# Delta-rule attention in one core: the order of VectorE's work in a slot, and who gates the output row

## The chip, the cores and the metric

The kernel runs on one core of a Trainium2 chip. The metric is the device time of one execution in microseconds. Every duration below comes from one profiled execution of the kernel before.

## The reference

Six residual layers act on x of shape (2, 2048, 256): a gated feed-forward, the delta-rule attention, the feed-forward again, a binary-weight layer, a state-space layer, and the binary layer again. The change is in the attention. For each head (16 heads of size 16) and each chunk of 64 tokens:

```python
q = l2norm(x @ Wq) / sqrt(K); k = l2norm(x @ Wk); v = x @ Wv; gate = x @ Wg
P = where(strict, (k_beta @ k.T) * L, 0)          # L: decays exp(g_i - g_j)
Ainv = I + P + P@P ... ; v = Ainv @ v; k_cumdecay = Ainv @ (k_beta * exp(g))
# scan over the chunks, with state S
attn = where(tril, (q @ k.T) * L, 0)
v_new = v - k_cumdecay @ S
o = (q * exp(g)) @ S + attn @ v_new
S = S * exp(g_last) + (k * exp(g_last - g)).T @ v_new
# afterwards
o = o * rsqrt(mean(o*o) + 1e-5) * norm_w;  o = o * silu(gate);  out = o @ Wo
```

The kernel works in chunks of 32 rows instead of 64, which is the same mathematics.

## The kernel before

The program is a row of phases: first feed-forward, gates, delta (the attention), feed-forward, binary, space, binary. Only `delta_sync`, `delta_vector` and `delta_gpsimd` are touched.

The 4096 rows are 32 tiles of 128 rows (64 from each sequence; four sub-chunks of 32 rows, two steps of the scan in time). The delta phase runs 40 slots, n = 0 to 39. It is a software pipeline written out by hand: in slot n the projections and normalised keys of tile n are made, the decays and the masked products of tile n-1 (`LAG_FORM`), the inverse is applied for tile n-6, the scan runs for tile Z = n-7 (`LAG_SCAN`), and the output projection runs for tile O = n-8 (`LAG_OUT`). `at(stage, t)` calls a stage if tile t exists. Each engine has its own loop over n, so the order of the calls in it is the order of its queue; engines meet only through semaphores.

**VectorE** (`delta_vector`, L1818 to L1845) has two kinds of work. The first is the triangular solve (`solve`, L1741): for each pair of tiles 58 steps, 29 (`HALF_SOLVE`) per slot, each of which waits for the step before it through `S.i_step`. Even slots do the first half, in which the operations grow from 30 columns to 240; odd slots the second, in which they shrink again. The second kind is the stages, put between the steps:

- `sum_qk` (L1695), sum of the squares of q and k; `scale_qk` (L1709), normalises q and k out of PSUM bank 4 into `QK`;
- `faded_q` (L1717), from PSUM bank 1; it waits for `f_kt`, which ScalarE's `keep_kq` (L1585, L1586) raises;
- `keep_gate` (L1701); `keep_within` and `keep_attn` (L1726, two operations each);
- the scan: `own_heads` (L1784) twice per slot, waiting for `s_b` from TensorE's `to_state` (L1474), and `new_state` (L1792, L1797) twice;
- the output: `sum_o` (L1803), `scale_o` (L1808), `add_o` (L1812), and for the first 12 tiles `new_stats` (L312, L313).

**GpSimd** (`delta_gpsimd`, L1900 to L1909): `fade_first` (L1882), `middle_state` (L1889), `fade_second` (L1894), `gate_o` (L1898), `decayed_k` (L1865), `kept_k` (L1875, two operations). All of them read SBUF. The last two wait for `scale_qk` through `p_kn`.

**TensorE** (`delta_tensor`, L1515 to L1531) is not touched. Its order in slot n is: `from_values`, `from_state` (L1442, L1461) for Z half 0, `project_qk(n)` (L1371), `to_state` (L1474) half 0, `turn_kq(n-1)` (L1401), `decays` (L1389, L1392), `from_values` and `from_state` half 1, `project_vg` (L1381), `to_state` half 1, `turn_o` (L1506), `apply` (L1427), `outputs` (L1492, L1497), `within` (L1411), `project_o` (L1512). The waits that matter:

```python
def project_qk(t):
    pe.wait_ge(S.p_in[t % 2], 16 * (t // 2 + 1))
    if t > 0:
        pe.wait_ge(S.p_kn, t)          # scale_qk(t - 1) has read bank 4
```

`turn_kq(t)` waits for `scale_qk(t)` too, and `outputs` for `keep_gate` and both halves of the state.

**ScalarE**, in slot n: `keep_y` (L1626) and `widen` (L1642) half 0, `squares(n)` (L1541), `keep_kq(n-1)`, DMA issues, `keep_y` half 1, `root_qk` (L1553, L1554), `widen` half 1, `keep_v`, `sigmoid_g`, `exp_decays`, `keep_ot`, `keep_wt`, `keep_ut`, `keep_o`, `spread_vk`, `root_o`.

**SyncE** sends and fetches the scratch tensors: `keys_out` writes the scaled keys of a tile and `keys_in` brings them back in another layout, seven tiles deep.

Of the kernel before, what the change touches and what calls it, by code (L numbers as in the profile page):

```python
# [8 lines left out]
ALU = mybir.AluOpType  # L9
# [10 lines left out]
BLK = 4  # L20
NT = 32
# [28 lines left out]
def bcast_last(ap, n):  # L50
    return ap.unsqueeze(2).to_broadcast([ap.shape[0], ap.shape[1], n])
# [6 lines left out]
def heads(ap):  # L58
    return ap.rearrange("p (h d) -> p h d", d=HD)
# [223 lines left out]
AHEAD = 3  # L283
# [902 lines left out]
LAG_FORM, LAG_PAD, LAG_APPLY, LAG_SCAN, LAG_OUT = 1, 5, 6, 7, 8  # L1186
# [67 lines left out]
def solve_count(m, k):  # L1254

    return m * (2 * HALF_SOLVE + 1) + 1 + k
# [7 lines left out]
def at(stage, t, *more):  # L1264

    if 0 <= t < NT:
        stage(t, *more)


def turned_in(e, B, xT, S, t):  # L1270

    b = t // BLK
    e.wait_ge(S.xt_out[b % 2], 32 * (b // 2 + 1))
    src = bass.AP(tensor=B.xT_dram, offset=t * P, ap=[[NT * P, P], [P * NT * P, KD], [1, P]])
    e.dma_start(xT[t % 2].rearrange("p (k n) -> p k n", k=KD), src).then_inc(S.p_in[t % 2], 16)
# [14 lines left out]
def delta_sync(e, B, M, S, run):  # L1290
    Pd, Td = B.P_dram, B.T_dram

    def rows_in(t):
        if t >= 2:
            e.wait_ge(S.p_vg, t - 1)
            turned_in(e, B, M.xT, S, t)

    def decays_in(t):
        if t >= 2:
            e.wait_ge(S.f_d, t - 1)  # L1300
            e.wait_ge(S.f_qgt, t - 1)
        e.wait_ge(S.g_out, 48)
        for part in range(2):
            rows = bass.AP(tensor=B.g_dram, offset=part * NT * NH * P + t * NH * P, ap=[[512, 4], [1, 512]])
            e.dma_start(M.G[t % 2][4 * part:4 * part + 4, :], rows).then_inc(S.f_in[t % 2], 16)
        for g in range(G2):
            src = bass.AP(tensor=B.eg_dram, offset=(t * NH + 8 * g) * P, ap=[[P, 8], [0, HD], [1, P]])
            e.dma_start(M.egT[t % 2][:, g * P:(g + 1) * P], src).then_inc(S.f_in[t % 2], 16)

    def keys_out(t):  # L1310
        e.wait_ge(S.p_kd, t + 1)
        dst = bass.AP(tensor=B.Kd_dram, offset=t * P * DM, ap=[[SUB, P], [SUB * P, 8], [1, SUB]])
        e.dma_start(dst, M.Kd_tok[t % 2].rearrange("p (n c) -> p n c", n=8)).then_inc(S.k_out[t % 2], 16)

    def keys_in(t):

        e.wait_ge(S.k_out[t % 2], 16 * (t // 2 + 1))
        if t >= 2:
            e.wait_ge(S.k_in[t % 2], 64 * (t // 2))
        if t >= 7:  # L1320
            e.wait_ge(S.s_b, 2 * (t - 6))
        for r in range(4):
            src = bass.AP(tensor=B.Kd_dram, offset=t * P * DM + 8192 * r, ap=[[SUB, SUB], [1024, 8], [1, SUB]])
            dst = M.Kd[t % 7][SUB * r:SUB * r + SUB, :].rearrange("p (n c) -> p n c", n=8)
            e.dma_start(dst, src).then_inc(S.k_in[t % 2], 16)

    def pair_in(m):
        e.wait_ge(S.i_out[0], 64 * (m + 1))
        e.wait_ge(S.i_out[1], 64 * (m + 1))
        if m >= 2:  # L1330
            e.wait_ge(S.i_back[m % 2], 16 * (m // 2))
        whole = bass.AP(tensor=Pd, offset=m * 131072, ap=[[1024, P], [1, 1024]])
        e.dma_start(M.PR[m % 2], whole).then_inc(S.i_in[m % 2], 16)

    def pair_back(m):
        back = bass.AP(tensor=Td, offset=m * 131072, ap=[[1024, P], [1, 1024]])
        e.wait_ge(S.i_step, solve_count(m, 2 * HALF_SOLVE))
        e.dma_start(back, M.PR[m % 2]).then_inc(S.i_back[m % 2], 16)

    def within_out(t):  # L1340
        e.wait_ge(S.f_pt, t + 1)
        for r in range(4):
            dst = bass.AP(tensor=Pd, offset=t * 65536 + r * 16384, ap=[[SUB, SUB], [1024, NH], [1, SUB]])
            e.dma_start(dst, M.PT[SUB * r:SUB * r + SUB, :].rearrange("p (n i) -> p n i", n=NH)).then_inc(S.i_out[t % 2], 16)

    for n in range(SLOTS):
        at(rows_in, n + 1)
        at(decays_in, n)
        at(keys_out, n - 1)
        at(keys_in, n - 2)  # L1350
        at(within_out, n - LAG_FORM)
        if n % 2 == 0:
            if 0 <= (n - 2) // 2 < NT // 2:
                pair_in((n - 2) // 2)
            if 0 <= n - 5 < NT:
                inverse_in(e, B, M, S, n - 5, (0, 1), S.i_diag)
        elif 0 <= (n - 5) // 2 < NT // 2:
            pair_back((n - 5) // 2)
            inverse_in(e, B, M, S, n - 5, (0, 1), S.i_diag)
# [327 lines left out]
def delta_vector(v, own, B, M, S, run):  # L1687
# [117 lines left out]
    def scale_o(t):  # L1805
        v.wait_ge(S.o_rs, t + 1)
        v.wait_ge(S.o_sb, t + 1)
        v.tensor_tensor(heads(M.o_sb), heads(M.o_sb), bcast_last(M.o_rs, HD), ALU.mult).then_inc(S.o_mul, 1)  # L1808

    def add_o(t):  # L1810
        v.wait_ge(S.o_w, t + 1)
        v.tensor_tensor(B.X[:, t, :], bank[7][:, DM:], B.X[:, t, :], ALU.add).then_inc(S.o_x, 1)  # L1812
# [5 lines left out]
    for n in range(SLOTS):  # L1818
        Z, O = n - LAG_SCAN, n - LAG_OUT
        at(own_heads, Z, 0)  # L1820
        solve(n, 0, 1)
        at(new_state, Z, 0)
        solve(n, 1, 3)
        at(sum_qk, n)
        solve(n, 3, 6)
        at(faded_q, n - LAG_FORM)
        solve(n, 6, 10)
        at(scale_qk, n)
        solve(n, 10, 11)
        at(own_heads, Z, 1)  # L1830
        solve(n, 11, 12)
        at(new_state, Z, 1)
        solve(n, 12, 15)
        at(keep_gate, n)
        solve(n, 15, 21)
        at(sum_o, Z)
        solve(n, 21, 24)
        at(keep_within, n - LAG_FORM)
        solve(n, 24, 25)
        at(keep_attn, n - LAG_FORM)  # L1840
        solve(n, 25, 29)
        at(scale_o, Z)
        at(add_o, O)
        if O < AHEAD * BLK:
            at(new_stats, O)  # L1845


def delta_gpsimd(g, own, B, M, S, run):
# [34 lines left out]

    def middle_state(t):
        g.wait_ge(S.s_e, 2 * t + 1)
        g.wait_ge(S.s_bm, 2 * t + 1)
        if t > 0:
            g.wait_ge(S.s_wide, 2 * t)
        g.tensor_tensor(M.S1, M.E0, M.Bm, ALU.add).then_inc(S.s_1, 1)  # L1889
# [3 lines left out]
        g.wait_ge(S.s_1, t + 1)  # L1893
        g.tensor_tensor(states(M.E1), states(M.S1), bcast_last(end[:, 4:8], SUB), ALU.mult).then_inc(S.s_e, 1)  # L1894

    def gate_o(t):
        g.wait_ge(S.o_mul, t + 1)
        g.tensor_tensor(M.o_sb, M.o_sb, M.gate[t % 9], ALU.mult).then_inc(S.o_gate, 1)  # L1898

    for n in range(SLOTS):  # L1900
        Z = n - LAG_SCAN
        at(fade_first, Z)
        at(middle_state, Z)
        at(fade_second, Z)
        at(gate_o, n - LAG_OUT)
        at(decayed_k, n)
        at(kept_k, n)
        if n in (SLOTS - 4, SLOTS - 3):
            first_factors(g, own, B, S, 1, n - (SLOTS - 4))  # L1909

# [273 lines left out]
```

## Time and profile before

| | us |
|---|---|
| profiled execution, device time | 1235.57 |
| its span on the core | 1233.8 |
| the three timed runs | 4384.79, 3293.92, 1240.54 |
| their median | 3293.92 |
| delta phase, about | 222 to 825 of the span |

The span is what the profile shows, from the first to the last instruction. Over the whole span TensorE is busy 84%, VectorE 75%, ScalarE 49%, GpSimd 33%; these are averages over phases with different limits, and the delta phase, half of the span, has to be read by itself.

### The profile page before, as it was taken

The numbers are of one execution on the slowest core, as the hardware profiler recorded it, in microseconds if no ns is written. First come the engines' busy times: TensorE is split into PE (matmuls) and PEld (weight loads), VectorE is DVE, ScalarE is ACT, GpSimd is POOL, SyncE is SP. The second block draws the span as 40 slices with busy tenths as digits, with TensorE's granted clock in tenths as the row PEclk, the third lists the DMA queues.
The fourth block names the chain that finished last, engine by engine and source line by source line (L and its number), as shares of the span: only waits on it lengthen the run. The fifth ranks groups of instructions, "written<-read, shape, count | busy, mean of one in ns | idle before, by whom it ended". The sixth has DMA issues, their size and how long they took to land. (4 is left out here: it accounts for less than half of the span.)

```text
span 1233.8 us, 38552 instructions
## 1 busy us (share of the span) xinstructions
PE 1038.0 (84%) x15542; PEld 739.6 (60%) x15542; DVE 925.7 (75%) x2403; ACT 599.7 (49%) x1614; POOL 405.8 (33%) x580
## 2 busy tenths in 40 slices
PE   2999977778888888788898886679999798799878
PEld 2888853445555565555565565458888574355455
DVE  3777736358999999999988988528776345899853
ACT  2433336434767676777766765554332452101052
POOL 2666630311222121222121211216665257400055
PEclk9999988886999999999989987779999798899979
DMA  9000013244444444444434443100000034954013
GB/s 251 20 2 1 1 27 141 69 87 98 104 101 103 94 97 86 102 106 104 100 78 99 102 94 71 42 2 1 1 1 1 18 74 104 232 160 115 1 35 103
DMA packets 282625, 93.31 MB, mean 76 GB/s; under 512 B 208976, under 2 KB 275408, under 8 KB 282448
## 3 DMA queue, kind: packets, MB, share of 16 engines
q1 hardware_dynamic: 247056, 84.03, 28.3%
q10 hardware_dynamic: 35392, 6.82, 2.9%
q8 instruction: 123, 2.02, 0.7%
q14 instruction: 54, 0.44, 0.1%
HBM read 56.20 MB, written 30.41 MB: 70 GB/s over the span
## 5 line engine op out<-in xcount | busy, mean ns | idle before, releaser
L1777 DVE TENSOR_TENSOR delta_tmp<-delta_PR 128x130 f32<-128x130 f32 (+12 forms) x416 | 152.9, 368 | 9.4
L1774 DVE TENSOR_TENSOR delta_PR<-delta_PR,delta_tmp 128x130 f32<-128x130 f32 (+12 forms) x416 | 152.1, 366 | 9.3
L1889 POOL TENSOR_TENSOR delta_S<-delta_E,delta_Bm 128x128 f32<-128x128 f32 x32 | 15.3, 477 | 282.2 <-issue 273.3
L1427 PE MATMUL psum<-delta_T,delta_pad 128*32 128x128 f32 x2048 | 81.2, 325 | 31.9 <-DMA delta_T<-inverse_scratch 31.4
L1626 ACT ACTIVATE delta_y<-psum 32x128 f32<-32x128 f32 x256 | 68.7, 268 | 80.1 <-PE psum L1461 58.2
L1427 PEld LDWEIGHTS psum<-delta_T,delta_pad 128*32 128x32 f32 x2048 | 69.6, 131 | 41.7 <-DMA delta_T<-inverse_scratch 38.2
L507 POOL TENSOR_TENSOR ffn_H<-ffn_hid,ffn_H 128x512 fp32r<-128x512 f32 x48 | 61.8, 1292 | 57.5 <-DVE ffn_H L473 57.5
L1642 ACT ACTIVATE delta_wide<-delta_S 32x128 f32<-32x128 f32 x256 | 78.2, 306 | 3.2
L507 POOL TENSOR_TENSOR first_H<-first_hid,first_H 128x512 fp32r<-128x512 f32 x48 | 61.7, 1292 | 53.9 <-DVE first_H L473 53.9
L1411 PE MATMUL psum<-delta_MV,delta_KT 32*32 32x128 f32 x2048 | 68.9, 287 | 10.6 <-ACT delta_E L1576 10.6
L1865 POOL TENSOR_TENSOR delta_VK<-delta_QK,both_eg 128x256 f32<-128x256 f32 x32 | 20.8, 650 | 156.6 <-DVE delta_QK L1709 156.5
L1411 PEld LDWEIGHTS psum<-delta_MV,delta_KT 32*32 32x32 f32 x2048 | 58.9, 112 | 22.2 <-ACT delta_E L1576 15.5
L1371 PE MATMUL psum<-both_w_in,delta_xT 128*128 128x512 f32 x128 | 67.0, 648 | 3.3 <-DVEq L172 2.1
L439 ACT ACTIVATE first_silu<-psum 128x512 f32<-128x512 f32 x48 | 28.7, 599 | 84.2 <-PE psum L392 84.2
L439 ACT ACTIVATE ffn_silu<-psum 128x512 f32<-128x512 f32 x48 | 28.8, 599 | 81.3 <-PE psum L392 81.3
L641 PE MATMUL psum<-w_bin,binary_XT 128*128 128x256 f32 x256 | 67.4, 408 | 0.0
L312 DVE BATCH_NORM_STATS2 ln_stats<-X 128x6 f32<-128x256 f32 x128 | 54.1, 423 | 17.0 <-DMA X<-in_x 14.4
L1474 PEld LDWEIGHTS psum<-delta_y,delta_Kd 32*32 32x32 f32 x2048 | 22.9, 110 | 71.0 <-ACT delta_y L1626 71.0
L1381 PE MATMUL psum<-both_w_in,delta_xT 128*128 128x512 f32 x128 | 64.4, 627 | 0.0
L710 DVE TENSOR_SCALAR binary_Y<-psum 128x512 f32<-128x512 f32 x32 | 22.1, 692 | 54.5 <-PE psum L641 54.5
L392 PE MATMUL psum<-first_XT,w_gate 128*128 128x512 f32 x192 | 54.6, 407 | 3.7 <-DVE first_XT L461 3.7
L641 PEld LDWEIGHTS psum<-w_bin,binary_XT 128*128 128x128 f32 x256 | 48.4, 199 | 14.2 <-issue 8.4
(282 smaller groups left out, 2594.8 us busy)
## 6 DMA issues: line engine op xcount, KB each, us to landing
within_scratch<-delta_PT SPq DMA_DIRECT2D x128, 64.0 KB, 1.9
delta_PR<-within_scratch SPq DMA_DIRECT2D x16, 512.0 KB, 4.3
inverse_scratch<-delta_PR SPq DMA_DIRECT2D x16, 512.0 KB, 3.0
space_T<-taps_scratch SPq DMA_DIRECT2D x8, 1024.0 KB, 5.9
X<-taps_scratch SPq DMA_DIRECT2D x8, 1024.0 KB, 8.9
X<-in_x SPq DMA_DIRECT2D x32, 128.0 KB, 10.2
turned_scratch<-gates_XT SPq DMA_DIRECT2D x16, 256.0 KB, 2.3
delta_xT<-turned_scratch SPq DMA_DIRECT2D x32, 128.0 KB, 3.8
```

Source lines behind the costliest of these rows:

```text
L392: i = pe.matmul(bank[:], w[:, k * HID + m * P:k * HID + (m + 1) * P].bitcast(F32R), M.XT[b % 2][hl][k].bitcast(F32R), start=(k == 0 and hl ...
L439: a.activation(M.silu[n % 3], B.bank[n % 2][:], ACT.Silu, scale=1.0 / 127.0).then_inc(S.silu, 1)
L507: g.tensor_tensor(lo.bitcast(F32R), M.hid[n % 3], hi, ALU.subtract).then_inc(S.hid_lo, 1)
L641: i = pe.matmul(o[:, j * DM:(j + 1) * DM], M.XT[b % 3][k][:, (2 * h + j) * P:(2 * h + j + 1) * P], B.w_bin[:, k * DM:(k + 1) * DM], start= ...
L1371: i = pe.matmul(bank[4][:], M.xT[t % 2][:, k * P:(k + 1) * P], M.w_in[:, k, 0:512], start=(k == 0), stop=(k == 1))
L1381: i = pe.matmul(bank[5][:], M.xT[t % 2][:, k * P:(k + 1) * P], M.w_in[:, k, 512:1024], start=(k == 0), stop=(k == 1))
L1411: mm = pe.matmul(kk[g][rows, q * P:(q + 1) * P], M.KT[rows, g * P + SUB * q:g * P + SUB * q + SUB], M.MV[rows, (4 * g + q) * P:(4 * g + q ...
L1427: i = pe.matmul(bank[3][SUB * c:SUB * c + SUB, (2 * w + g) * P:(2 * w + g + 1) * P], M.pad[:, from_c:from_c + SUB], M.T[t % 2][:, h * P:(h ...
L1626: i = a.activation(dst, heads(bank[6][rows, half * P:(half + 1) * P]), ACT.Copy)
L1642: i = a.activation(states(M.wide[half])[rows, :, SUB * c:SUB * c + SUB], states(X)[rows, :, :], ACT.Copy)
L1774: i = v.tensor_tensor(after, after, t3, ALU.add)
L1777: i = v.tensor_tensor(t3, column.to_broadcast([P, j, n_after]), row.to_broadcast([P, j, n_after]), ALU.mult)
```

## The change

In the slot loop of `delta_vector`, `scale_qk` goes from a third of the way through the solve to behind it, and `keep_within` and `keep_attn` go behind it too. `faded_q`, `sum_qk` and `add_o` (now of tile O-1, a slot later) go ahead of the solve, directly behind the first half of the state update. Ten places inside the solve where a stage stood become four. `gate_o` moves from GpSimd to VectorE, at the slot's end. GpSimd's `fade_first` for the next tile goes to the end of its slot, and its `middle_state` waits for the second operation of VectorE's state update (`s_x`) rather than the first (`s_bm`). SyncE's `keys_out` and `keys_in` come one slot later.

```diff
--- before.py
+++ after.py
@@ delta_sync
-        at(keys_out, n - 1)
-        at(keys_in, n - 2)
+        at(keys_out, n - 2)
+        at(keys_in, n - 3)
@@ delta_vector
+    def gate_o(t):
+        v.wait_ge(S.o_mul, t + 1)
+        v.tensor_tensor(M.o_sb, M.o_sb, M.gate[t % 9], ALU.mult).then_inc(S.o_gate, 1)
+
     for n in range(SLOTS):
         Z, O = n - LAG_SCAN, n - LAG_OUT
         at(own_heads, Z, 0)
-        solve(n, 0, 1)
         at(new_state, Z, 0)
-        solve(n, 1, 3)
+        at(add_o, O - 1)
+        at(faded_q, n - LAG_FORM)
         at(sum_qk, n)
-        solve(n, 3, 6)
-        at(faded_q, n - LAG_FORM)
-        solve(n, 6, 10)
+        if O - 1 < AHEAD * BLK:
+            at(new_stats, O - 1)
+        solve(n, 0, 9)
+        at(own_heads, Z, 1)
+        solve(n, 9, 10)
+        at(new_state, Z, 1)
+        solve(n, 10, 15)
+        at(keep_gate, n)
+        solve(n, 15, 25)
+        at(sum_o, Z)
+        solve(n, 25, 29)
         at(scale_qk, n)
-        solve(n, 10, 11)
-        at(own_heads, Z, 1)
-        solve(n, 11, 12)
-        at(new_state, Z, 1)
-        solve(n, 12, 15)
-        at(keep_gate, n)
-        solve(n, 15, 21)
-        at(sum_o, Z)
-        solve(n, 21, 24)
         at(keep_within, n - LAG_FORM)
-        solve(n, 24, 25)
         at(keep_attn, n - LAG_FORM)
-        solve(n, 25, 29)
         at(scale_o, Z)
-        at(add_o, O)
-        if O < AHEAD * BLK:
-            at(new_stats, O)
+        at(gate_o, Z)
+    add_o(NT - 1)
@@ delta_gpsimd
     def middle_state(t):
         g.wait_ge(S.s_e, 2 * t + 1)
-        g.wait_ge(S.s_bm, 2 * t + 1)
+        g.wait_ge(S.s_x, 2 * t + 1)
@@
-    def gate_o(t):
-        g.wait_ge(S.o_mul, t + 1)
-        g.tensor_tensor(M.o_sb, M.o_sb, M.gate[t % 9], ALU.mult).then_inc(S.o_gate, 1)
-
     for n in range(SLOTS):
         Z = n - LAG_SCAN
-        at(fade_first, Z)
         at(middle_state, Z)
         at(fade_second, Z)
-        at(gate_o, n - LAG_OUT)
         at(decayed_k, n)
         at(kept_k, n)
+        at(fade_first, Z + 1)
```

## Rows read from the trace of the kernel before

**Rows 1.** Windows of the delta phase: us, each engine's busy us, PEclk, DMA.

```profile
263.00:307.00 44.00, 33.12 (x401) 20.18 (x399) 39.27 (x114) 17.80 (x51) 5.17 (x10) 0.77 0.41 89
...
323.00:729.00 406.00, 345.51 (x9334) 232.57 (x9333) 375.48 (x1093) 286.44 (x911) 90.76 (x168) 0.97 0.46 97
```

**Rows 2.** VectorE's waits from 323 to 729: total us, times, longest.

```profile
DVE delta_Bm L1784 <- PE psum L1474: 5.6, 12, 0.9
```

**Rows 3.** Timeline: the solve's first steps without and with GpSimd beside them.

```profile
263.65 0.69 DVE L1763 SCALAR_TENSOR_TENSOR delta_PR<-delta_PR 128x30 f32<-128x30 f32 x3
...
595.28 1.07 DVE L1763 SCALAR_TENSOR_TENSOR delta_PR<-delta_PR 128x29 f32<-128x29 f32 x2
...
595.58 0.73 POOL L1898 TENSOR_TENSOR delta_o_sb<-delta_o_sb,delta_gate 128x256 f32<-128x256 f32 x1
```

**Rows 4.** Timeline of VectorE: two chained steps, then a stage between two steps.

```profile
604.64 0.39 DVE L1777 TENSOR_TENSOR delta_tmp<-delta_PR 128x220 f32<-128x220 f32 x1
...
605.07 0.39 DVE L1774 TENSOR_TENSOR delta_PR<-delta_PR,delta_tmp 128x220 f32<-128x220 f32 x1
605.37 0.41 DVE L1803 TENSOR_REDUCE delta_o_ss<-delta_o_sq 128x16 f32<-128x256 f32 x1
605.70 0.38 DVE L1777 TENSOR_TENSOR delta_tmp<-delta_PR 128x228 f32<-128x228 f32 x1
```

**Rows 5.** Groups of VectorE, 222 to 830: count | busy us, mean ns | idle before.

```profile
L1777 DVE TENSOR_TENSOR delta_tmp<-delta_PR 128x130 f32<-128x130 f32 (+12 forms) x416 | 152.9, 368 | 9.4
L1774 DVE TENSOR_TENSOR delta_PR<-delta_PR,delta_tmp 128x130 f32<-128x130 f32 (+12 forms) x416 | 152.1, 366 | 9.3
...
L1763 DVE SCALAR_TENSOR_TENSOR delta_PR<-delta_PR 128x29 f32<-128x29 f32 (+1 forms) x48 | 23.8, 521 | 0.6
L1709 DVE TENSOR_TENSOR delta_QK<-psum,delta_rs 128x512 f32<-128x512 f32 x32 | 22.0, 687 | 8.1 <-ACT delta_rs L1554 7.8 <-issue 0.2
L1695 DVE TENSOR_REDUCE delta_ssq<-delta_sq 128x32 f32<-128x512 f32 x32 | 21.6, 676 | 9.4 <-ACT delta_sq L1541 9.4
L1784 DVE TENSOR_TENSOR delta_Bm<-psum,consts 128x128 f32<-128x128 f32 x64 | 18.1, 283 | 18.1 <-PE psum L1474 18.1
...
L1808 DVE TENSOR_TENSOR delta_o_sb<-delta_o_sb,delta_o_rs 128x256 f32<-128x256 f32 x32 | 13.4, 419 | 2.5 <-ACT delta_o_rs L1561 2.5
...
L1768 DVE SCALAR_TENSOR_TENSOR delta_PR<-delta_PR 128x29 f32<-128x29 f32 (+1 forms) x48 | 11.7, 273 | 1.1
L312 DVE BATCH_NORM_STATS2 ln_stats<-X 128x6 f32<-128x256 f32 x12 | 5.1, 427 | 0.4
```

**Rows 6.** Timeline of early slots: scaled keys to projection, turned keys to faded_q.

```profile
230.45 0.69 DVE L1709 TENSOR_TENSOR delta_QK<-psum,delta_rs 128x512 f32<-128x512 f32 x1 [0.65 <-ACT delta_rs L1554]
...
231.29 1.95 PE L1371 MATMUL psum<-both_w_in,delta_xT 128*128 128x512 f32 x4 [1.19 <-DVE delta_QK L1709]
...
242.28 0.60 PE L1401 MATMUL psum<-consts,delta_QK 128*128 128x128 f32 x4
...
244.54 0.42 DVE L1717 TENSOR_TENSOR delta_QgT<-psum,delta_egT 128x256 f32<-128x256 f32 x1 [0.74 <-ACT delta_KT L1586]
```

**Rows 7.** Timeline of a full slot's start: TensorE from the outputs on, VectorE's wait.

```profile
689.08 0.65 PE L1492 MATMUL psum<-delta_y,delta_AT 128*32 128x64 f32 x32 [1.01 <-DVE delta_gate L1701]
...
693.72 1.98 PE L1371 MATMUL psum<-both_w_in,delta_xT 128*128 128x512 f32 x4
...
695.64 0.45 PE L1474 MATMUL psum<-delta_y,delta_Kd 32*32 32x32 f32 x32
...
696.02 0.66 PE L1401 MATMUL psum<-consts,delta_QK 128*128 128x128 f32 x4
...
696.17 0.29 DVE L1784 TENSOR_TENSOR delta_Bm<-psum,consts 128x128 f32<-128x128 f32 x1 [0.85 <-PE psum L1474]
```

**Rows 8.** Window (columns as in rows 1) and timeline of a stretch at granted clock 0.50.

```profile
285.00:289.00 4.00, 4.00 (x50) 2.65 (x43) 3.69 (x12) 0.00 (x0) 0.22 (x1) 0.50 0.03 4
...
287.38 3.06 PE L1371 MATMUL psum<-both_w_in,delta_xT 128*128 128x512 f32 x4
```

## Prediction

> **What bounds the kernel now.** I read the windows by phase first. In the part of the delta phase where every stage runs, 323 to 729, 24 slots take 406.0 us, 16.92 each; VectorE is busy 375.5 of them (92%) and TensorE 345.5 (85%) [rows 1]. So VectorE's queue sets the slot, with TensorE close behind. Then the waits: what VectorE loses to others in that stretch is small, 12 waits of at most 0.9 us for `to_state` among them [rows 2]. Last, the timeline, for what is inside the 92%: the solve's first operations are stretched when GpSimd reads SBUF beside them. Three of them take 0.69 us together in slot 4, where GpSimd is quiet, and in slot 24, with `gate_o` of 0.73 us beside them, two take 1.07 [rows 3].
>
> **The change part by part.** I give costs per slot; there are 24 full slots, n = 8 to 31.
>
> *Contention, removed.* The four solve lines are busy 152.9 + 152.1 + 23.8 + 11.7 = 340.5 us [rows 5], 10.64 per slot. The 48 operations of L1763 have the size of those of L1768 (273 ns), yet average 521 [rows 5]; without a neighbour three take 0.69 us, 0.23 to 0.25 each [rows 3]. That excess is 48 x 0.27 = 13 us, 0.4 per slot. The wider steps beside `decayed_k` and `kept_k`, and `new_state`, I put at as much again (the other SBUF-to-SBUF steps of the same half slots), so 0.9 per slot from the solve and 0.3 from `new_state`: 1.2 removed. Bounds: 0.4, L1763 alone, and 2.0. Behind the change GpSimd's operations lie beside PSUM-reading stages, which show no stretch (`scale_qk` 687 ns, `own_heads` 283 [rows 5]), except for `scale_o` and `gate_o`; I leave 0.3 for those two.
>
> *Interleaving, lost.* A chained step starts 0.43 us after a step of 0.39: its duration and 0.04. With `sum_o` (0.41) between them the two steps are 0.63 apart, so the stage costs 0.20 [rows 4]: an operation that waits for nothing starts about 0.08 before the end of the one ahead of it, and hides the 0.03 to 0.04 of the next wait. Each place where a stage breaks the chain is worth 0.11. Ten places become four, `new_state` now stands directly behind the `own_heads` it reads, and `gate_o` behind `scale_o`: 8 x 0.11 = 0.9 us per slot. Bounds: 0 and 1.1.
>
> The Trainium skill says otherwise (VectorE: DVE Perf Modes, section The DRAIN you can't avoid): chained VectorE operations pay the flush with or without a semaphore, so that the semaphore costs nothing extra. By it this term would be 0. The trace here shows the 0.11, and I go by the trace.
>
> *gate_o, added to VectorE.* It has the shape of `scale_o`, 0.42 us [rows 5]; 0.34 net of the 0.08. What it takes from GpSimd (0.73, [rows 3]) is worth nothing there, since GpSimd is busy 90.8 of 406 us [rows 1].
>
> These three almost cancel: -1.2 + 0.3 + 0.9 + 0.34 = +0.3 us. They are not what decides. That is where the moved stages meet the other engines.
>
> *scale_qk at the slot's end: a wait.* `project_qk(n)` waits for `scale_qk(n-1)`, and in TensorE's queue `to_state` half 0 and `turn_kq(n-1)` stand behind `project_qk(n)`. Before, `scale_qk(n-1)` was done a third of the way through its own slot, and full slots show no such wait. Now I count from its start, S.
>
> - `scale_qk` 0.69, then 0.15 to the projection (230.45 to 231.29 is 0.84 [rows 6]): `project_qk` at S + 0.84.
> - `to_state` 1.92 later, `turn_kq` 0.38 after that [rows 7]: S + 2.76 and S + 3.14.
> - `own_heads` can run 0.53 after `to_state` starts (695.64 to 696.17 [rows 7]): S + 3.29.
> - `faded_q` can run 2.26 after `turn_kq` starts (242.28 to 244.54 [rows 6]), because `keep_kq`'s three operations on ScalarE come between: S + 5.40.
>
> VectorE's own work between S and `faded_q` is 0.60 (`scale_qk`), 4 x 0.34 (`keep_within`, `keep_attn`), 0.45 + 0.34 (`scale_o`, `gate_o`) and 0.3 of contention, so that `own_heads` could start at 3.05 and waits 0.24 there. Then 0.32 + 0.20 + 0.34 (`own_heads`, `new_state`, `add_o`) lead to S + 4.15, and `faded_q` waits 1.25 more. Before, `own_heads` was three solve steps, `sum_qk` and three more ahead of `faded_q`, which covered it.
>
> *The new slot.* From `faded_q` at S + 5.40: 0.34 for it, 0.60 for `sum_qk`; 29 solve steps without contention, 9.75 + 24 x 0.034 - 5 x 0.08 = 10.2; `own_heads` and `new_state` half 1 at 0.20 each, `keep_gate` and `sum_o` at 0.33 each. The next `scale_qk` starts at 5.40 + 0.94 + 10.2 + 1.06 = **S + 17.6**. It hides nothing else: `keep_gate` ends by S + 13.5 (15 steps of 0.43 behind `sum_qk`), and from the outputs to the next `project_qk` TensorE needs 4.64 (689.08 to 693.72 [rows 7]), which gives 18.2, below 17.6 + 0.84 = 18.4. It is close: a late TensorE adds to the wait.
>
> *The rest.* `fade_first` at the slot's end, the later wait of `middle_state`, and `keys_out`/`keys_in` a slot later are covered: `kept_k(n-2)` was done a slot ago, and its keys are read seven slots on. I cost them at nothing. `within_out` comes some 3 us later in SyncE's queue, and `inverse_in` behind it; `apply` may start up to 2 us later in every second slot, which the 13.5 of `keep_gate` covers.
>
> *The sum.* Full slots: 24 x 17.6 = 422.4, and `new_stats` (0.43 and its short second operation, about 0.6 [rows 5]) in 12 of them, 7.2: 429.6 against 406.0, **+23.6**. Slot 7 took 16.0 (307 to 323, between the windows) and takes 17.6: **+2**. Slots 4 to 6 have the solve without the scan; 44.0 us [rows 1], 14.7 each. There the chain to `faded_q` is S + 4.9 and the slot 4.9 + 0.94 + 10.2 + 0.33 and two places more to chain, 16.6: **+6**. In slots 0 to 3 `sum_qk` now stands behind `faded_q`, and ScalarE's `root_qk` delays the gate behind it, about 0.5 each: **+2**. Slots 32 to 39 have no projection and no such wait; contention less and `gate_o` more, **0**, within 3 either way. Together +34: 1235.6 + 34 = **1270 us**. This is set against the profiled execution's own time, 1235.57, which is 0.4% below the fastest of the three timed runs; their median of 3293.92 is 2.7 times the span, and nothing in the trace could account for it, so I don't forecast against it.
>
> **The rivals.**
>
> *The moved work is covered after all* (the other side: not slower). If `project_qk` and `keep_kq` are ready when VectorE comes, the slot is VectorE's own work, 15.8 + 0.3 = 16.1, and 16.4 with the statistics' share: 24 x -0.5 = -12, and -2 for the rest: 1222. For it: VectorE is busy 92%, and the contention is real [rows 1, 3]. Against it: the order of the queues leaves no way round; it needs S to `faded_q` at 3.6 us or less where the rows add up to 5.4. If contention removed is at its upper bound of 2.0 too, 1205. Chance 0.15.
>
> *Chained steps cost nothing.* The wait is as forecast but the lost interleaving is free: six places in the solve, 0.66 in each of 28 slots, 18 less: 1252. This is also the Trainium skill's rule above. Against it: [rows 4]. Chance 0.08.
>
> *TensorE's clock falls at the new wait.* TensorE now stands still for about 2 us at each slot's start, on top of the waits for the inverse and the gate. The granted clock was 0.97 in the full slots and 0.77 in slots 4 to 6 [rows 1], where TensorE waits more. At 0.50 (1.2 GHz) `project_qk` took 3.06 [rows 8] rather than 1.98 [rows 7], and it stands in the new chain with `to_state` and `turn_kq`: about 1.5 per slot. In half of the slots that is +18 to +20, in all +36: 1290 and 1306. Chance 0.15.
>
> **How the numbers follow.** Forecast 0.62, at 1270, its own range 1256 to 1288 (contention and interleaving at their bounds while the wait holds: the part before `faded_q` absorbs half of them). What a measurement of this kernel can tell from no change is about 2%, 1211 to 1260. Faster by over 2% is the part of the first rival with contention at its bound, 0.07. Slower is nearly nine tenths of the forecast and the clock's case, 0.55 + 0.15 = 0.70, 0.69 after rounding the parts. The rest, 0.24, is within. The range that leaves out 2 in 10 runs from 1240, between the first rival and the second, to 1298, inside the clock's case.
>
> **What would show it.** In the profile after: `own_heads` with an idle time for TensorE's L1474 in most slots, and `faded_q` with one of about 1.3 us for ScalarE's L1586 (each step right); `project_qk` waiting for VectorE's L1709; the L1763 group at about 0.25 us each (contention gone); full slots of 17.6 us. If `faded_q` doesn't wait, I'm wrong on the chain, and the time is near 1222. If the full slots are above 18.2, TensorE's clock or its lateness is in the chain, and the granted clock of the full slots tells which.

## The result, and the profile after

The changed kernel takes 1302.0 us (1301.1 to 1306.4 in 4 runs), against 1236.8 and 1240.5 for the kernel before: 1.0518 times as long, 95% interval 1.047 to 1.0567. The two executions of 3.3 and 4.4 ms in the list of the kernel before did not come again in any later run of it and are left out of the comparison. The forecast was slower, 1270, with a range to 1298: the sign was right, and the +34 us forecast are about half of what came. The span grew by 66.7 us, from 1233.8 to 1300.5.

Where it went, by the first `own_heads` of each slot in the two timelines: up to slot 7 +14.3 us (307.5 to 321.8), slot 7 +2.2, the 24 full slots +43.8 (406.0 to 449.9), the drain (slots 32 to 39, in which the pipeline empties) and what follows +6.3. The windows of the start and of the full slots, with the columns of [rows 1]:

```profile
263.00:322.00 59.00, 35.14 (x408) 20.24 (x405) 40.60 (x118) 18.81 (x52) 5.15 (x12) 0.74 0.34 70
339.00:788.00 449.00, 350.90 (x9330) 237.03 (x9316) 372.41 (x1113) 285.87 (x908) 64.81 (x142) 0.95 0.41 88
```

VectorE's busy time hardly moved, 375.5 to 372.4 us, though it took `gate_o` over; what it sits idle in the full slots grew from 30.5 to 76.6 us. The groups of VectorE from 222 to 890 (count | busy us, mean ns | idle before) show what the change was made for:

```profile
L1777 DVE TENSOR_TENSOR delta_tmp<-delta_PR 128x130 f32<-128x130 f32 (+12 forms) x416 | 145.7, 350 | 11.8
L1774 DVE TENSOR_TENSOR delta_PR<-delta_PR,delta_tmp 128x130 f32<-128x130 f32 (+12 forms) x416 | 145.5, 350 | 12.3
...
L1812 DVE TENSOR_TENSOR delta_o_sb<-delta_o_sb,delta_gate 128x256 f32<-128x256 f32 x32 | 15.6, 487 | 1.1
...
L1808 DVE TENSOR_TENSOR delta_o_sb<-delta_o_sb,delta_o_rs 128x256 f32<-128x256 f32 x32 | 14.5, 453 | 2.7 <-ACT delta_o_rs L1561 2.7
...
L1763 DVE SCALAR_TENSOR_TENSOR delta_PR<-delta_PR 128x29 f32<-128x29 f32 (+1 forms) x48 | 10.7, 250 | 1.1
```

Against [rows 5], L1763 fell from 23.8 to 10.7 us, L1777 and L1774 by 7.2 and 6.6: 26.9 us of stretch gone from the solve, 0.84 per slot; the two `new_state` lines fell by 8.8 us together, from 27.3 to 18.5. `scale_o` and `gate_o`, which now lie beside GpSimd, take 453 and 487 ns, where `scale_o` took 419.

Who waits, from 310 to 760 (total us, times, longest; VectorE, then TensorE, then ScalarE, and last ScalarE in the kernel before):

```profile
DVE delta_QgT L1717 <- ACT delta_KT L1586: 29.5, 24, 1.5
DVE delta_Bm L1784 <- PE psum L1474: 23.7, 33, 3.1
```

```profile
PE psum L1371 <- DVE delta_QK L1709: 31.9, 19, 6.1
PE psum L1427 <- DMA delta_T<-inverse_scratch: 30.8, 12, 3.6
PE psum L1474 <- ACT delta_y L1626: 23.9, 12, 2.8
PE psum L1492 <- DVE delta_gate L1701: 14.3, 12, 2.4
```

```profile
ACT delta_y L1626 <- issue: 34.0, 12, 3.8
```

```profile
ACT delta_y L1626 <- issue: 14.0, 8, 2.8
```

VectorE's two lines, and TensorE's first, are the chain of the forecast. TensorE's third and ScalarE's are not in it: in 12 slots, every second one, `keep_y` comes late, and `to_state` behind it. "Issue" stands there for ScalarE's own `inverse_in`, which is ahead of `keep_y` half 1 in its queue and waits until `pair_back` has landed. The kernel before had this wait too, in 8 slots and 14.0 us. The slots alternate, most regularly from slot 22 on: 18.0, 17.5, 19.5, 17.6, 19.8, 17.7 and 20.7 us. One boundary shows both, the start of slot 24 and what follows, in the timeline:

```profile
636.43 0.69 DVE L1709 TENSOR_TENSOR delta_QK<-psum,delta_rs 128x512 f32<-128x512 f32 x1
...
637.27 1.95 PE L1371 MATMUL psum<-both_w_in,delta_xT 128*128 128x512 f32 x4 [0.23 <-DVE delta_QK L1709]
...
637.81 3.06 SPq L1344 DMA_DIRECT2D within_scratch<-delta_PT  x4
...
639.15 0.45 PE L1474 MATMUL psum<-delta_y,delta_Kd 32*32 32x32 f32 x32
...
639.68 0.29 DVE L1784 TENSOR_TENSOR delta_Bm<-psum,consts 128x128 f32<-128x128 f32 x1 [0.32 <-PE psum L1474]
...
640.92 0.51 SPq L1338 DMA_DIRECT2D inverse_scratch<-delta_PR  x1
...
641.81 0.43 DVE L1717 TENSOR_TENSOR delta_QgT<-psum,delta_egT 128x256 f32<-128x256 f32 x1 [1.17 <-ACT delta_KT L1586]
```

```profile
643.97 0.91 ACTq L1287 DMA_DIRECT2D delta_T<-inverse_scratch  x2
644.98 1.11 ACT L1626 ACTIVATE delta_y<-psum 32x128 f32<-32x128 f32 x4 [3.21 <-issue]
...
646.67 0.29 DVE L1784 TENSOR_TENSOR delta_Bm<-psum,consts 128x128 f32<-128x128 f32 x1 [1.23 <-PE psum L1474]
```

The first block is the forecast's chain to within 0.04 us: from S = 636.43 the projection comes at +0.84, `to_state` at +2.72, `own_heads` at +3.25 with a wait of 0.32, `faded_q` at +5.38 with one of 1.17. The second block is what I missed. The solve of the pair was done by 636.52, but SyncE sends it back (L1338) only at 640.92, behind the four transfers of `within_out`, which themselves waited for `keep_within`. ScalarE's `inverse_in` waits for that landing until 643.97, `keep_y` half 1 starts only behind it, at 644.98, after 3.21 us in which ScalarE computed nothing, and `own_heads` half 1 waits 1.23.

### The profile page after: what moved, and what is told of

Its sections match the earlier page's. It is cut to its first block and busy times, and to the rows that moved or that the text cites. A ratio compares the mean times of both kernels' runs of the same rounds, so it can differ in the third digit from the quotient of the medians.

```text
span 1300.5 us, 38552 instructions
## 1 busy us (share of the span) xinstructions
PE 1045.3 (80%) x15542; PEld 744.8 (57%) x15542; DVE 924.6 (71%) x2435; ACT 600.8 (46%) x1614; POOL 373.1 (29%) x548
## 5 line engine op out<-in xcount | busy, mean ns | idle before, releaser
L1774 DVE TENSOR_TENSOR delta_PR<-delta_PR,delta_tmp 128x130 f32<-128x130 f32 (+12 forms) x416 | 145.5, 350 | 12.3
L1777 DVE TENSOR_TENSOR delta_tmp<-delta_PR 128x130 f32<-128x130 f32 (+12 forms) x416 | 145.7, 350 | 11.8
L1427 PE MATMUL psum<-delta_T,delta_pad 128*32 128x128 f32 x2048 | 84.0, 332 | 38.6 <-DMA delta_T<-inverse_scratch 37.6
L1371 PE MATMUL psum<-both_w_in,delta_xT 128*128 128x512 f32 x128 | 72.0, 691 | 51.4 <-DVE delta_QK L1709 49.3
L1474 PE MATMUL psum<-delta_y,delta_Kd 32*32 32x32 f32 x2048 | 30.7, 200 | 51.0 <-ACT delta_y L1626 51.0
L1411 PEld LDWEIGHTS psum<-delta_MV,delta_KT 32*32 32x32 f32 x2048 | 58.0, 111 | 23.4 <-ACT delta_E L1576 16.9
L1371 PEld LDWEIGHTS psum<-both_w_in,delta_xT 128*128 128x128 f32 x128 | 24.4, 212 | 74.2 <-issue 71.6
L312 DVE BATCH_NORM_STATS2 ln_stats<-X 128x6 f32<-128x256 f32 x128 | 54.0, 422 | 16.8 <-DMA X<-in_x 14.6
L1381 PE MATMUL psum<-both_w_in,delta_xT 128*128 128x512 f32 x128 | 62.7, 612 | 0.0
```

What stands on the lines that cost most here:

```text
L1371: i = pe.matmul(bank[4][:], M.xT[t % 2][:, k * P:(k + 1) * P], M.w_in[:, k, 0:512], start=(k == 0), stop=(k == 1))
L1381: i = pe.matmul(bank[5][:], M.xT[t % 2][:, k * P:(k + 1) * P], M.w_in[:, k, 512:1024], start=(k == 0), stop=(k == 1))
L1411: mm = pe.matmul(kk[g][rows, q * P:(q + 1) * P], M.KT[rows, g * P + SUB * q:g * P + SUB * q + SUB], M.MV[rows, (4 * g + q) * P:(4 * g + q ...
L1427: i = pe.matmul(bank[3][SUB * c:SUB * c + SUB, (2 * w + g) * P:(2 * w + g + 1) * P], M.pad[:, from_c:from_c + SUB], M.T[t % 2][:, h * P:(h ...
L1474: i = pe.matmul(bank[6][rows, DM + (2 * s + g) * SUB:DM + (2 * s + g + 1) * SUB], M.Kd[t % 7][rows, (4 * g + q) * SUB:(4 * g + q + 1) * SU ...
L1774: i = v.tensor_tensor(after, after, t3, ALU.add)
```

## The experiments

All ratios are against the kernel before, measured beside. "Full slots" is the time from the first `own_heads` of slot 8 to that of slot 32, 406.0 before and 449.9 after; I read it from each timeline. "At half clock" is time at the lower of TensorE's two levels, (1 - granted clock) x 2 x the slot's length, summed over the full slots: 23 us in the kernel before, 41 in the changed one.

### The two stages that wait, and SyncE's queue

**pair_back ahead of within_out, nothing else.**

```diff
@@ delta_sync, changed kernel
+        if n % 2 == 1 and 0 <= (n - 5) // 2 < NT // 2:
+            pair_back((n - 5) // 2)
         at(within_out, n - LAG_FORM)
...
         elif 0 <= (n - 5) // 2 < NT // 2:
-            pair_back((n - 5) // 2)
```

> The changed kernel with one edit in SyncE's queue: in odd slots pair_back goes ahead of within_out. The changed kernel's slots alternate, about 17.6 us when no pair goes back and 18.5 to 20.7 when one does. Theory (queue order): the solve now ends before keep_within, but pair_back stands behind within_out (issue 3.06 us), so the inverse lands about 2.5 us later; ScalarE's inverse_in waits for it (3.21 us ahead of keep_y), and to_state half 1 and own_heads half 1 are late. Then the even slots fall to about 17.8, the drain loses some of its length too: 14 slots by 1.7 us, 1302 to about 1278. Rival (TensorE's clock or its lateness makes the long slots): no change, 1300 to 1304, and the slots still alternate.

Measured 1290.7, ratio 1.0419 (1.0376 to 1.0462). ScalarE's wait fell from 34.0 us to 0.4, and the alternation went; full slots 440.2. So the mechanism is there, but half of the time that it should have given back was not: TensorE now waited 34.0 us for `keep_gate`, where it had waited 14.3. The drain gave back what it had lost: from slot 32's first `own_heads` to the end of the span is 505.6 us here, 511.3 in the changed kernel, 505.0 before.

**faded_q behind six solve steps, nothing else.**

```diff
@@ delta_vector, changed kernel
-        at(faded_q, n - LAG_FORM)
         at(sum_qk, n)
...
-        solve(n, 0, 9)
+        solve(n, 0, 6)
+        at(faded_q, n - LAG_FORM)
+        solve(n, 6, 9)
```

> The changed kernel with faded_q moved back behind six solve steps, nothing else. Theory: its wait of 1.17 us per slot for keep_kq is covered; odd slots fall from 17.6 to 16.4, even slots keep most of their length because there own_heads half 1 waits for ScalarE, which waits for the inverse: 1302 - 14 x 1.2 - 14 x 0.3 = about 1281. Rival (every wait is additive): all slots fall by 1.2, 1268. Rival (the wait is only moved to the next stage): 1300.

Measured 1289.1, ratio 1.0403 (1.0365 to 1.0442). The slots that no other wait lengthens fell to 16.7 with `new_stats` and 16.2 without; every second slot stayed at 18.5 to 20.9. The wait is real, and behind it stands the other one.

**Both.**

> The two edits together, pair_back ahead of within_out and faded_q behind six solve steps; scale_qk stays at the slot's end. Theory: what is left is the wait of own_heads half 0 (0.3 us), so all full slots are near 16.5 to 16.8, against 16.9 of the kernel before: 1302 - 24 - 33 = about 1245, the same as before within 1.5%. Rival (clock): above 1270.

Measured 1262.5, ratio 1.018 (1.0129 to 1.0231). The two together give 39.5 us where each alone gave 11 and 13: as long as one wait stands, the other is partly hidden in it. But 1262.5 is 17 above the 1245 expected. Thirteen full slots are 16.2 to 16.8; the eleven others are 17.1 to 20.0. `apply` waits for the inverse (26.4 us in 13 slots), and behind one such wait, of 3.33 us, its 64 matmuls take 3.64 us rather than the 1.95 of the next slot.

**scale_qk behind ten steps, all else as changed.**

```diff
@@ delta_vector, changed kernel
         solve(n, 9, 10)
+        at(scale_qk, n)
         at(new_state, Z, 1)
...
         solve(n, 25, 29)
-        at(scale_qk, n)
```

> The changed kernel with only scale_qk moved back, behind ten solve steps; all other moves stay, the SyncE order too. Theory: project_qk no longer waits for VectorE, TensorE runs ahead as before, so own_heads half 0 and faded_q wait little; contention by decayed_k and kept_k comes back (0.5 us per slot). Odd slots near 16.8. pair_back is still behind within_out, which may keep 1 to 2 us in the even ones: 1250 to 1265. Rival (the position of faded_q alone costs the time): 1295 or more.

Measured 1298.0, ratio 1.0479 (1.0445 to 1.0513). This is the miss that mattered. Undoing the move that my chain starts from gave 4 us of 64. The 4 us hide two large parts that cancel. Against the changed kernel the first `own_heads` comes 12.2 us earlier (309.6), but the full slots take 11.7 us more (461.6). `project_qk` no longer waited, but TensorE's idle time only changed its place. `apply` waited 51.1 us for the inverse, in 13 slots, up to 5.5, and 88 us were at half clock. `faded_q` still waited 21.5 us in 22 slots, since, as I read it, it follows `to_state` by the length of ScalarE's `keep_kq` whoever lets `to_state` go.

**SyncE's queue alone, whole.** `inverse_in` goes ahead of `within_out` too, in even slots.

```diff
@@ delta_sync, changed kernel (on top of pair_back ahead of within_out)
+        if n % 2 == 0 and 0 <= n - 5 < NT:
+            inverse_in(e, B, M, S, n - 5, (0, 1), S.i_diag)
         at(within_out, n - LAG_FORM)
...
-            if 0 <= n - 5 < NT:
-                inverse_in(e, B, M, S, n - 5, (0, 1), S.i_diag)
```

> The changed kernel with SyncE's queue alone mended: in odd slots pair_back goes ahead of within_out, in even slots inverse_in does. VectorE, GpSimd, TensorE and ScalarE as changed. Theory: within_out waits for keep_within, which the change put at the slot's end, and what stands behind it (pair_back, inverse_in) made apply wait up to 4.8 us, ScalarE up to 3.8 us, and TensorE's clock fall behind that wait. With both ahead of it the full slots are the 17.5 (18.1 with new_stats) of the wait chain through scale_qk and faded_q, 24 x 17.8 = 427 against 449.9 measured, and less time at half clock: 1275 to 1282. With pair_back alone moved it was 1290.7. Rival (the wait chain on VectorE makes all of it): as with pair_back alone, 1288 or more.

Measured 1294.4, ratio 1.0456 (1.0428 to 1.0483): the rival's number. `apply` did not wait for the inverse any more, and yet nothing was won, since TensorE came earlier to `outputs` and waited for `keep_gate` there, 57.8 us in 22 slots, up to 3.6, where the changed kernel had 14.3 us in 12. Half-clock time is 58 us. From slot 11 to slot 19 its slots alternate between 18.4, where the granted clock stays at full, and 19.1, where it is at half for 3.4 us behind that wait.

**The same with faded_q behind six steps.**

> The same mending of SyncE's queue and faded_q behind six solve steps. Theory: no wait of apply for the inverse, no clock lost behind it; full slots 16.7 to 16.8, or 16.2 to 16.6 without new_stats, 24 x 16.6 = 398 against 418.1 with pair_back and faded_q alone: 1240 to 1245. Rival (the half clock comes from the wait of project_qk for scale_qk, not from apply's): 1258 to 1264, half clock as before in 40 of 400 us.

Measured 1248.6, ratio 1.01 (1.0063 to 1.0137). Full slots 410.1. Five sixths of the 64 us are gone; slots are 15.9 to 16.9 where the clock stays up, 17.5 to 18.4 where it falls.

**And with scale_qk behind ten steps on top.**

> The run with SyncE's queue mended and faded_q behind six steps (1248.6), and scale_qk moved back behind ten steps as well: every stage whose place made a wait is back, the new places of the PSUM reads, the add and gate_o stay. Theory: the wait of project_qk (30.1 us in 21 slots) goes, own_heads half 0 then waits little; decayed_k and kept_k stretch the solve again by 0.5 us per slot: between 1232 and 1244. Rival (scale_qk's place was not a cost at all, only the stages behind it): no change, 1246 to 1251.

Measured 1257.6, ratio 1.0155 (1.0114 to 1.0196). Taking the last wait of the forecast away made it 9 us slower; the intervals of the two ratios just overlap, but the parts are clear. The first `own_heads` comes 15.3 us earlier (302.1 against 317.4) and the full slots take 20.6 us more (430.7 against 410.1). Without that wait TensorE's idle time stands in one place, 60.7 us in 22 waits for `keep_gate`, up to 4.2. With `scale_qk` late about as much idle time is in two places, 30.1 us ahead of `project_qk` and 27.4 for `keep_gate`. The mean granted clock from 340 to 750 is 0.91, against 0.96 with `scale_qk` late.

### TensorE's clock

If the clock is what the long wait costs, then work in that wait should give the time back. The fill is such work: matmuls that nobody reads, into a quarter of PSUM bank 6 that the phase does not use, between `apply` and `outputs`, 12 of them in the first of these runs, 8, 14 or 10 in the others. The added wait, for `own_heads` half 1, keeps them out of the bank while VectorE reads it. The traces show 2.94 us for 12 of them, 2.05 for 8, 2.50 for 10 and 3.39 for 14, nearly twice what the expectations below put them at.

```diff
@@ delta_tensor
         at(apply, n - LAG_APPLY)
+        if 0 <= Z and n < NT:
+            pe.wait_ge(S.s_bm, 2 * Z + 2)
+            for _ in range(12):
+                pe.matmul(bank[6][:, 384:512], B.ident, B.ident, start=True, stop=True)
         at(outputs, Z)
```

> mended_scale_early (1257.6) with 12 matmuls of 128x128x128 that nobody reads, into an unused quarter of PSUM bank 6, between apply and outputs of slots 7 to 31, where TensorE waited 60.7 us in 22 slots for keep_gate. They cost about 1.7 us of TensorE's time in a wait of 2.8 us. Theory (TensorE's clock falls behind the one long wait and stretches apply's followers): time at half clock from 71.7 to under 40 us, full slots from 430.7 to about 412, 1238 to 1244. Rival (the waits are the cost and the clock only goes along): 1256 to 1270, as the added work can only delay.

Measured 1240.0, ratio 1.0033 (1.0015 to 1.0051), 17.6 us faster than the same kernel without the added work; full slots 412.8 against 430.7. The same window of the kernel without the fill and then with it:

```profile
340.00:750.00 410.00, 343.09 (x8836) 232.08 (x8835) 363.40 (x1062) 269.22 (x859) 65.14 (x136) 0.91 0.43 92
```

```profile
340.00:750.00 410.00, 394.81 (x9796) 285.42 (x9798) 377.64 (x1106) 281.34 (x898) 65.71 (x139) 0.99 0.45 95
```

A mean of 0.91 is (1 - 0.91) x 2 x 410 = 74 us at the lower level, 1.2 GHz; with the fill no full slot shows any. In the kernel without it one such place reads:

```profile
562.49 1.08 PE L1493 MATMUL psum<-delta_y,delta_AT 128*32 128x64 f32 x32 [2.71 <-DVE delta_gate L1702]
...
564.35 3.64 PE L1412 MATMUL psum<-delta_MV,delta_KT 32*32 32x128 f32 x64
```

`within` (L1412) takes 3.64 us there, 1.95 in the next slot; `project_o`, the state's products and `project_qk` stand behind it. The Trainium skill (TensorE: Matmul & The Clock Gate, Part 1) says that the throttled state is the default and that activity releases it. The trace agrees: 2.71 us of idle ahead of the slow stretch, and no slow stretch in the full slots once the idle time is filled.

**The fill with scale_qk late.**

> sync_and_faded (1248.6, 30.7 us at half clock) with 8 such matmuls, about 1.1 us, at the same place, where TensorE waited 27.4 us in 23 slots. Theory (clock): the six or seven long slots of 17.9 to 18.5 go to 16.7, about 1238 to 1243. Rival (the wait there is too short to hold them: 1.2 us, the work comes on the path): 1249 to 1256.

Measured 1239.7, ratio 0.9997 (0.9964 to 1.003). Full slots 400.2, below the 406.0 of the kernel before, and none at half clock. The 2.05 us of fill are longer than the waits for `keep_gate` that they stand in, 1.2 us on average; the rest came out of the wait of `project_qk` behind them, 30.1 to 14.9 us.

**The fill in the kernel before.**

> The kernel before with 8 such matmuls at the same place; apply waited 23.8 us and outputs 24.6 us there. Theory: seven of its full slots show 3.4 us at half clock; with them at full clock some 5 to 8 us less, 1228 to 1234. Rival (TensorE is close behind VectorE there, so the added 1.1 us comes on the path in the slots without a wait): 1240 to 1250.

Measured 1259.6, ratio 1.019 (1.0152 to 1.0228), the rival's side and worse than it said. `apply` waits for its transfer there in 14 slots, so that the added work begins late and comes on the path; `sum_o` then waits for ScalarE's squares of the outputs, 17.1 us in 12 slots. The clock fell all the same, for 21 us of the full slots against 23 without the fill. The fill's 2.05 us stand here in waits of 1.3 us on average (24.6 us in 19 slots), and there is no wait of `project_qk` behind them to take up the rest. That this decides whether a fill pays is my reading of the kernels here; no run varies the length of the fill in one of them.

**The fill in sync_order**, which leaves VectorE's and GpSimd's part of the change whole: the price of the forecast's chain nearly by itself. What remains beside it is the fill's own wait for `own_heads`, 7.1 us in 10 slots.

> sync_order (1294.4; 58.0 us of its full slots at half clock, 57.8 us of outputs waiting in 22 slots) with 14 matmuls that nobody reads between apply and outputs, about 2 us. All of the change on VectorE and GpSimd stays, with both its waits at the slot's start. Theory: without half clock every full slot is the chain from scale_qk to faded_q and the solve, 17.5 or 18.1 with new_stats, 428 in place of 450.4: 1269 to 1276. Rival (the chain costs more than I worked out, the clock less): 1285 or more.

Measured 1276.9, ratio 1.0343 (1.0315 to 1.0372). Full slots 432.5 us, all at full clock, where the forecast's sum had 429.6. Slots are mostly 17.6 and 17.8, or 18.1 and 18.4 with `new_stats`. From slot 32 to the end it takes 503.0 us, 505.0 in the kernel before. `late_filled` is this kernel with `faded_q` behind six steps and 8 matmuls instead of 14: its full slots take 32.3 us less. That is 1.35 us per slot, and more than the 26.5 us by which this kernel's full slots exceed those of the kernel before. So with the other two effects gone, the chain's price is that of the place of `faded_q`; a part of the 32.3 may be the longer fill.

### The other parts

**gate_o back on GpSimd, nothing else.**

> The changed kernel with gate_o alone back on GpSimd, at its old place behind fade_second. Theory: gate_o's 0.34 plus 0.1 leaves VectorE's stretch from scale_qk to own_heads, which has 0.3 us of wait anyway, so nothing is gained there; beside the solve's first steps GpSimd's 0.73 us lie beside faded_q's wait and sum_qk, which they do not stretch: no change, 1298 to 1305. Rival (gate_o's time on VectorE is on the path): 24 to 32 slots by 0.45, 1288 to 1291.

Measured 1305.0, ratio 1.0538 (1.0506 to 1.057), no difference from the changed kernel: on VectorE `gate_o` lies in the wait for `to_state`. With `gate_o` gone from there `own_heads` waits 35.6 us from 340 to 770, against 20.2.

**The kernel before with inverse_in ahead of within_out in even slots.**

> The kernel before with one edit: in even slots SyncE's inverse_in goes ahead of within_out. In the kernel before apply waited 23.8 us in 16 slots for that transfer, and outputs then waited for keep_gate all the same. Theory (keep_gate sets the slot there): the wait of apply turns into a wait of outputs, no change, 1230 to 1240. Rival (apply's wait is on the path in the slots of 17 to 18 us): 5 to 12 us less, 1225 to 1232.

Measured 1244.1, ratio 1.005 (1.0026 to 1.0074). The wait of `apply` became one of `outputs`, 24.6 to 45.7 us, and nothing was gained; if anything half a per cent was lost.

**scale_qk, keep_within and keep_attn ahead of the last four steps.**

```diff
@@ delta_vector, changed kernel, with faded_q behind six steps and, in delta_sync, inverse_in ahead of within_out in even slots
-        at(sum_o, Z)
-        solve(n, 25, 29)
         at(scale_qk, n)
         at(keep_within, n - LAG_FORM)
         at(keep_attn, n - LAG_FORM)
+        at(sum_o, Z)
+        solve(n, 25, 29)
```

> The changed kernel with scale_qk, keep_within and keep_attn put ahead of the last four solve steps (behind step 25, in that order, sum_o behind them), faded_q behind six steps, and inverse_in ahead of within_out in even slots. GpSimd's decayed_k and kept_k still lie beside the PSUM-reading stages. Theory: from scale_qk to own_heads VectorE now has 4.8 us of work of its own, more than the 3.3 that TensorE needs; no wait of the change is left and the contention is gone, so a full slot is about 16.0 (16.6 with new_stats): 24 x 16.3 = 391 against 406.0 before: 1215 to 1225, faster than both. Rival (contention was worth less than the lost interleaving and gate_o): 1235 to 1245.

Measured 1242.6, ratio 1.0041 (1.0018 to 1.0065), not the 1220 expected. The wait of `project_qk` is gone, but `sum_o` stands behind three more stages, and ScalarE waits 80.4 us for it in 24 slots, up to 3.9, with `keep_y` behind in its queue. `pair_back` is not moved in this kernel or in the next two.

**sum_o ahead of them, own_heads half 1 and keep_gate one step later.**

> As the run with scale_qk ahead of the last four solve steps, with sum_o put ahead of scale_qk (behind step 21), own_heads half 1 behind step 10, new_state behind 11, keep_gate behind 16. In that run ScalarE waited 80.4 us in 24 slots for sum_o before root_o, and keep_y stands behind root_o in its queue; that made to_state late (30.0 us). Theory (ScalarE's queue behind sum_o was the bound): those waits go, full slots 16.0 to 16.4, 1222 to 1232. Rival (TensorE's clock and the pair's way through memory bound it): 1236 to 1243.

Measured 1250.9, ratio 1.0108 (1.0081 to 1.0135). The 80.4 us are gone and it is slower: TensorE's waits for `keep_gate` grew from 31.6 to 46.1 us, half-clock time from 10 to 37 us. **With 10 matmuls of fill:**

> sum_o_early (1250.9; outputs waited 46.1 us in 23 slots, 37.5 us at half clock) with 10 such matmuls. Theory: its long slots of 17.8 to 18.9 fall to 16.1 to 16.8, full slots from 416.5 to about 400: 1233 to 1238, about the kernel before or just ahead. Rival (ScalarE's wait for the inverse, 21.3 us, bounds it): 1243 to 1250.

Measured 1267.1, ratio 1.0256 (1.0225 to 1.0287). Every second slot is 18 to 21 us, the others 16.1 to 16.5. The fill's 2.50 us stand in waits of 2.0 us on average (46.1 in 23 slots), with no wait of `project_qk` behind them, and ScalarE's wait for the pair that goes back late grew from 21.3 to 29.5 us. Whether these two make up the 16 us stays open; no run takes them apart.

### A version that beats both

`late_filled`, and in slots 0 to 6, before the scan runs, `scale_qk` behind ten steps:

```diff
@@ delta_vector, on top of late_filled
         solve(n, 9, 10)
+        if n < LAG_SCAN:
+            at(scale_qk, n)
         at(new_state, Z, 1)
...
-        at(scale_qk, n)
+        if n >= LAG_SCAN:
+            at(scale_qk, n)
```

> late_filled (1239.7) with scale_qk behind ten solve steps in slots 0 to 6 alone, where the wait of project_qk for it took 5 to 6 us each in slots 5 to 7 of the changed kernel and cost 10 us up to the first own_heads (317.7 against 307.6). Theory: the first own_heads comes at 305 to 309, full slots stay at 400: 1229 to 1233, 0.5% ahead of the kernel before. Rival (the pipeline's fill only shifts the time into slot 7 and 8): 1238 to 1241.

Measured 1225.2, ratio 0.9922 (0.9901 to 0.9942): 0.8% less than the kernel before, 5.9% less than the changed one. The first `own_heads` comes at 303.3, where it comes at 317.6 in `late_filled`; full slots are 399.9. In the changed kernel that start looked like this, a projection of 3.75 us behind an idle 6.54:

```profile
298.47 3.75 PE L1371 MATMUL psum<-both_w_in,delta_xT 128*128 128x512 f32 x4 [6.54 <-DVE delta_QK L1709]
```

## Why the prediction was right and wrong

**What bounds the kernel: right, but incomplete.** VectorE's queue sets the slot, but TensorE is idle for a part of each slot, and the sum did not ask where. In `mended_scale_early` it is idle in one piece and the clock falls to a mean of 0.91; in `sync_and_faded` the same amount in two pieces leaves 0.96.

**Contention: right.** 26.9 us came off the solve and 8.8 off `new_state`, 35.7 in 32 slots or 1.1 per slot, against 1.2 forecast. `scale_o` and `gate_o` are stretched by 0.10 per slot, where I had left 0.3. What the removed stretch is worth in time by itself no run shows. The Trainium skill (SBUF — State Buffer, Who interferes with whom) has it that a VectorE instruction with two SBUF inputs contends with a GpSimd instruction that reads SBUF, and one with at most one, outside the two-port modes, does not. The traces agree: L1763 averaged 521 ns before, when GpSimd worked beside most of these operations, and 250 after; `keep_within` and `keep_attn`, which read one operand from PSUM and now lie beside GpSimd, take 415 ns against 417 and 414.

**Interleaving: borne out.** The uncovered slots of `sync_order_filled2`, 17.6 to 17.8, match the 17.6 worked out with 0.11 per chained place. With chained steps free, as the rule weighed in the prediction has it, they would have been 16.9. That is agreement of a sum and no run of its own. The steps in the changed kernel's trace repeat the rows: around `sum_o` at 635.15 two steps start 0.49 us apart, the first lasting 0.25, and 0.30 apart where nothing is between, the first lasting 0.27; so the stage of 0.41 costs 0.21.

**gate_o: right.** Its move costs and gives nothing measurable.

**The wait chain: right in every link, and nearly in its price once alone.** At slot 24, S + 0.84, + 2.72, + 3.25, + 5.38 were forecast as 0.84, 2.76, 3.29, 5.40, and `faded_q` waits 1.2 us in all 24 full slots, for 1.25 forecast. Without the other two effects the full slots take 432.5 against 429.6; that kernel is 1276.9, the forecast was 1270. The forecast did not say that undoing one link does not undo the chain: `scale_qk_early` gave 4 us.

**"The rest ... I cost them at nothing": the step that failed.** The span grew by 33 us more than the forecast's 34: 20.3 of them in the full slots (449.9 against 429.6), 6.3 up to slot 7, 6.3 in the drain. The term for SyncE's queue stood at nothing, and it is not nothing. I had `within_out` 3 us later in SyncE's queue, looked at `inverse_in` for `apply` behind it, and found that covered. I did not take `pair_back` along, which stands in the same queue between them in odd slots, nor who waits for its landing on ScalarE. The trace of the kernel before already had this wait, 14.0 us in 8 slots; it became 34.0 in 12. From 1302.0 to `sync_order_filled2`'s 1276.9, 25 us, is this and the clock together; `pair_back_first` alone gave 11. How the rest divides between the two is not shown, since each depends on the other. The other parts of that sentence hold as far as `late_filled` shows, which keeps them all and has full slots of 400.2 us against 406.0. My sign of being wrong, full slots above 18.2, came (18.7 on average), but it named only TensorE.

**The clock: a rival with the wrong place.** I put the fall at the slot's start, behind the wait for `scale_qk`, gave it 0.15 and priced it by `project_qk`. In slots 5 to 7 it is there: `project_qk` waits about 6 us and then takes 3.75 us rather than 1.98, 5.3 us in three slots, which is most of what the first part has over the +8 forecast. Most of its +14.3 comes from the place of `scale_qk`: with that stage early and nothing else changed the first `own_heads` comes 12.2 us sooner. In the full slots the places that I looked at have it behind the longest wait, that for the inverse or for `keep_gate`, and the short wait at the slot's start, which splits the idle time, comes with a higher clock. `sync_and_faded` against `mended_scale_early` shows it: the full slots are 20.6 us shorter with that wait than without. The sum took the clock of the kernel before, 0.97, for a changed kernel whose slots are nearly 2 us longer with the same TensorE work; it came out at 0.95, 41 us at half clock against 23.

**The drain: the same miss.** +6.3, forecast 0 within 3. It is `pair_back` again: with that transfer ahead of `within_out` and nothing else, the drain and what follows are 0.6 us longer than before.

## What to carry to other kernels

When a stage moves in one engine's queue, follow every queue that waits for it past the first stage behind it: here the transfer next in that queue, and the engine that waits for its landing, cost 11 us of the 64 by themselves. Price an engine's idle time by where it collects: about 60 us in two waits per slot came with a mean granted clock of 0.96, in one wait with 0.91. Undo one link of a chain of waits and measure before believing in it; two mended together gave 39.5 us where one by one they gave 11 and 13.

## What the runs showed of the hardware that I had not expected

Work that nobody reads made a kernel faster: 12 matmuls in the wait ahead of `outputs` brought 1257.6 to 1240.0 us, and the mean granted clock from 340 to 750 from 0.91 to 0.99. Removing a real wait, that of `project_qk`, lengthened the full slots by 20.6 us (410.1 to 430.7), while the granted clock fell from 0.96 to 0.91. Such a fill is no general gain: 8 matmuls in the kernel before cost 22 us, and 10 in `sum_o_early` cost 16.
